# Two expert layers: every token through all eight experts, or each batch sorted by expert and only the chosen two computed

## The reference, cut to what matters

```python
logits = jnp.einsum('btd,ed->bte', x, router_w)          # 8 experts
top_vals, top_idx = jax.lax.top_k(logits, 2)
top_w = jax.nn.softmax(top_vals, axis=-1)
h = jnp.square(jax.nn.relu(jnp.einsum('nd,edh->enh', xf, w1)))   # 128 -> 256
y = jnp.einsum('enh,ehd->end', h, w2)                            # 256 -> 128
y_sel = y[idx_f, jnp.arange(N)[:, None]]
out = jnp.einsum('nk,nkd->nd', w_f, y_sel)                       # the two chosen
```

## Time and profile before

| | us |
|---|---|
| median of 3 runs | 1289.06 (1288.54 to 1292.21) |
| the profiled execution | 1291.25 |
| its span, first to last instruction | 1289.5 |
| granted TensorE clock, mean share of full | 0.96 |

### The profile page before, as it was taken

The page is one execution under the profiler, slowest core; times in us unless marked ns, Lnnn a source line. Parts: engine busy times, 40 slices in busy tenths (PEclk is TensorE's granted clock), DMA queues, the critical chain, the costliest instruction groups (busy, mean ns, idle before and its releaser), DMA issues.

```text
span 1289.5 us, 25719 instructions
## 1 busy us (share of the span) xinstructions
PE 1197.6 (93%) x10019; PEld 742.1 (58%) x10019; DVE 976.4 (76%) x2357; ACT 960.9 (75%) x1826; POOL 285.5 (22%) x326
## 2 busy tenths in 40 slices
PE   1779999998899999999999999999999999999998
PEld 1369999987434434444444444444444348999998
DVE  7575677766888898989898888988889814565654
ACT  1037777765158998888898888988888996777775
POOL 2032000003423333332332333332322100000000
PEclk9679999999569999999999999999999999999999
DMA  5100000000000000000000000000000000000000
GB/s 193 36 1 1 1 1 1 2 1 1 1 1 1 2 1 2 2 1 2 2 2 1 2 2 1 2 1 2 1 2 1 1 2 1 9 17 9 10 9 17
DMA packets 6134, 11.08 MB, mean 9 GB/s; under 512 B 1907, under 2 KB 3574, under 8 KB 5878
## 3 DMA queue, kind: packets, MB, share of 16 engines
q1 hardware_dynamic: 6014, 9.45, 2.1%
HBM read 7.28 MB, written 2.10 MB: 7 GB/s over the span
## 4 chain that ended last, share of the span: by engine, by line
PE 78%; DVE 13%; ACT 6%; issue 3%; DMA 0%; SPq 0%; ACTq 0%; DVEq 0%
PE acc L1280 17%; PE six L1115 17%; PE six L1251 10%; DVE mxp L947 8%; PE six L1103 6%; PE six L1105 5%; PE six L1104 5%; PE misc L1251 5%; ACT PB L645 3%; PE six L1264 2%; PE six L1217 1%; ACT SC L634 1%; PE six L1127 1%; PE six L1212 1%; PE misc L1103 1%
## 5 line engine op out<-in xcount | busy, mean ns | idle before, releaser
L947 DVE TENSOR_REDUCE mxp<-six 128x2 f32<-128x1024 f32 x512 | 598.8, 1219 | 75.4 <-PE six L1264 73.4
L645 ACT ACTIVATE PB<-six 128x512 f32<-128x512 f32 x681 | 384.9, 599 | 60.7 <-PE six L1251 36.9
L1280 PE MATMUL acc<-PB,Vg 128*32 128x256 f32 x4096 | 328.0, 392 | 16.3 <-ACT SC L634 16.3
L1264 PE MATMUL six<-K,Q 32*128 32x512 f32 x1024 | 264.1, 519 | 14.4 <-DVE mxp L947 9.7
L1251 PE MATMUL six<-Q,K 32*128 32x512 f32 x681 | 272.5, 498 | 0.1
L1115 PEld LDWEIGHTS six<-w2s,PB 128*128 128x128 f32 x2048 | 248.2, 192 | 11.3 <-ACT PB L547 0.7
L1115 PE MATMUL six<-w2s,PB 128*128 128x128 f32 x2048 | 249.3, 275 | 0.1
L850 DVE SCALAR_TENSOR_TENSOR x<-six,wexp,x 128x128 f32<-128x128 f32 x512 | 144.2, 345 | 134.9 <-PE six L1115 134.2
L541 ACT ACTIVATE PB<-six 128x512 f32<-128x512 f32 x256 | 151.2, 599 | 114.8 <-PE six L1105 104.4
L645 ACT ACTIVATE PB<-misc 128x512 f32<-128x512 f32 x343 | 205.4, 599 | 23.2 <-PE six L1251 17.1
L1251 PEld LDWEIGHTS six<-Q,K 32*128 32x128 f32 x681 | 107.9, 183 | 142.7 <-ACT PB L645 73.4
(11 more groups left out here) (225 smaller groups left out, 1094.7 us busy)
## 6 DMA issues: line engine op xcount, KB each, us to landing
x<-in_x SPq DMA_DIRECT2D x4, 512.0 KB, 5.1
SC<-in_w_om SPq DMA_DIRECT2D x1, 2048.0 KB, 14.6
out<-x SPq DMA_DIRECT2D x8, 256.0 KB, 2.0
VH<-in_w SPq DMA_DIRECT2D x1, 1024.0 KB, 9.2
Vg<-in_wqs SPq DMA_DIRECT2D x1, 256.0 KB, 8.0
Vg<-in_wks SPq DMA_DIRECT2D x1, 256.0 KB, 7.4
cst<-in_cst SPq DMA_DIRECT2D x1, 81.5 KB, 3.4
nwb<-in_nw SPq DMA_DIRECT2D x1, 64.0 KB
```

Of the source, the lines that this page charges most:

```text
L645: act.activation(PB[:, s % 3, j, :], scores, ACT.Exp).then_inc(G_("act_taken"), 1)
L947: dve.reduce_max(dst, taken_slot("max", s, i).rearrange("p (a n) -> p a n", a=2), AX.X).then_inc(G_("max_taken"), 1)
L1264: ins = pe.matmul(slot[:, c * BLK:(c + 1) * BLK], Q[rows, G % NG, t * P:(t + 1) * P], K[rows, G % NG, th * BLK:(th + 1) * BLK], start=True ...
L1280: ins = pe.matmul(acc[RB * j:RB * (j + 1), n], Vg[:, G % 2, t, j, :], PB[:, s % 3, j, n], start=(t == 0 and half == 0), stop=(t == TPB - 1 ...
```

## The change

Each expert layer now takes a whole batch (1024 tokens) at a time and computes only the two chosen experts.

**Routing a batch** (`rows`, `batch_top_two`, `batch_rank`, `batch_places`, `batch_weights`). VectorE normalises the 8 x 128 rows into `hbs`, TensorE turns them and multiplies with the router, VectorE takes the best two. TensorE counts with nine products (a triangle of ones, `tri`, and `ones`) how many (token, expert) pairs stand ahead of each pair, and VectorE computes from that a place in a list that is sorted by expert and in which each expert starts at a multiple of 128. The list has RT = 23 tiles of 128 lines, which is enough for 2 x 1024 pairs with any choice. POOL then sends the rows with 16 indirect DMAs of 128 rows (64 KB) each to `xs` in device memory (`send`), whose lines were set to zero before.

**The tiles.** SyncE loads the 23 tiles back in 6 groups (`load_lines`). TensorE turns each tile, multiplies it with the `w1` of the tile's expert (one fp32 product of 256 columns), turns the result (two transposes) and multiplies with `w2` (two fp32 products of 128 columns). Which expert that is, TensorE reads from memory into registers (`find_experts`, a TENSOR_LOAD for 4 tiles), and these address the weights. The tiles go in 12 pairs a batch, 48 steps a layer, with relu on VectorE (`relu_pair`) and the square and copies on ScalarE. SyncE stores the results to `yd` (`keep_lines`).

**Results.** POOL fetches them with 16 indirect DMAs a batch (`fetch_batch`), and VectorE adds them with their weights (`add_results`, 16 instructions of 128 columns a batch).

**Where it stands.** In the first layer batches 0, 1 and 2 are routed before the first tile (`experts_begin`), batch 3 beside the tiles of batch 0. The results of batches 0 and 1, attention's statistics for them and its first two norms and four projections lie beside the tiles of batches 2 and 3; the results of batches 2 and 3 are added within attention (`late_results`). In the second layer batches 0 and 1 are routed beside the last group of attention (`routed_late`), 2 and 3 beside the first tiles. `attention_end` now stands ahead of the second layer, with nothing beside it. Results of batches 1 to 3 are added after the last tile.

`w1` is no longer split and is loaded later, and the three-product form is gone from the experts (attention keeps it).

```diff
+RT = (2 * L + E * (P - 1)) // P
+TG = 4
+RGROUPS = -(-RT // TG)
+PAIRS = -(-RT // 2)
...
+            def send(f, b):
+                n = sparse_index(f, b)
+                pl.wait_ge(G_("dest_ready"), n + 1)
...
+                for i in range(TPB):
+                    for k in range(2):
+                        pl.indirect_dma_start(xs[b], bass.IndirectOffsetOnAxis(ap=dest[:, b, k, i:i + 1], axis=0),
+                                              hbs[:, b, i, :], None).then_inc(G_(f"sent{b}"), 16)
...
             low_part(2, 0)
-            split_out(0, 0)
             low_part(2, 1)
-            for t in range(1, 4):
+            fetch_start(0, 2)
+            for i in range(4):
+                fetch(0, 2, i)
+            for t in range(4):
                 split_out(0, t)
+            for i in range(4, TPB):
+                fetch(0, 2, i)
+            fetch_batch(0, 3)
             pl.wait_ge(*act_taken("v", 1))
...
-            low_part(3, 0)
-            for n in range(1, NBLK):
-                low_part(3, n)
+            for b in range(B):
+                send(1, b)
+            for b in range(B):
+                fetch_batch(1, b)
...
+            def experts_begin():
+                rms_norm(*RMS_GROUPS[0])
+                rms_norm(*RMS_GROUPS[1])
+                rows(0, 0)
+                rms_norm(*RMS_GROUPS[2])
+                batch_top_two(0, 0)
+                batch_weights(0, 0)
+                batch_places(0, 0)
+                rows(0, 1)
+                rms_norm(*RMS_GROUPS[3])
+                batch_top_two(0, 1)
+                rows(0, 2)
+                batch_places(0, 1)
+                batch_weights(0, 1)
+                batch_top_two(0, 2)
+                batch_places(0, 2)
+                batch_weights(0, 2)
...
+            def lines_hidden(f, b, q):
...
+                for r in range(2 * q, min(RT, 2 * q + 2)):
+                    ins = pe.matmul(big[:, n % 2, r % 2 * HID:(r % 2 + 1) * HID],
+                                    hTs[:, group % 2, r % TG * P:(r % TG + 1) * P], w1s[:, ds(expert_at[b, r], HID)],
+                                    start=True, stop=True)
...
+                for s in range(PAIRS * B):
+                    b, q = divmod(s, PAIRS)
+                    if q % 2 == 0 and s + 2 < PAIRS * B:
+                        turn_lines(f, *divmod(s // 2 + 1, RGROUPS))
+                    elif q % 2 and s + 3 < PAIRS * B:
+                        find_experts(f, *divmod((s + 3) // 2, RGROUPS))
+                    lines_hidden(f, b, q)
+                    if s:
+                        units_turned(f, *divmod(s - 1, PAIRS))
+                    if s >= 2:
+                        lines_result(f, *divmod(s - 2, PAIRS))
...
             pe.wait_ge(G_("max_taken"), len(DR))
+            for e in range(6):
+                attention_end(e)
             experts(1)
```

796 lines of the change are left out of this document (537 added, 259 removed).

## The result

The changed kernel takes **1270.77 us** (median of 3 runs, 1270.16 to 1273.85) against 1289.06: the ratio is 0.9858, with a 95% interval of 0.9823 to 0.9892. It is faster, by 18 us (1.4%) where 47 were forecast. A second measurement of the same kernel gave 1272.63, ratio 0.9865 (0.9845 to 0.9884). The profiled execution spans 1272.0 us. On other chips variants of this kernel are much slower than the kernel before; the last experiments are about that.

What follows compares the result with a forecast made beforehand. TensorE was taken to bound the expert layers and attention. Front +42, first layer -78, lead-in +9, attention +12 and second layer -32 sum to -47 us on a 1289.5 span: 1242 us, range 1190 to 1310.

Steps and rivals of the forecast that it cites:

- Attention, the step that failed: Attention's last group: two routings add 9.2 us to a nearly full TensorE, ScalarE's copies fall away, so 4 us.
- Attention, the lumps: Attention: VectorE's additions and statistics come in lumps longer than two PSUM slots cover (2.4 us), 1 us each, 8 us.
- (a): Expert layers: 24 register loads a layer at 0.7 us each cost 17 us, with 0 to 48 possible.
- (b): Expert layers: register instructions beside each pair's products cost 0.2 us a pair, 9 us a layer, with 0 to 47 possible.
- register work is hidden: Rival, expert layers: register loads and instructions fall to a third or nothing, -35 to -52 us, 1190 to 1207; chance 0.15.
- register work stalls TensorE: Rival, expert layers: loads at 2.0 us and 0.57 us a pair more, 96 us, giving 1338 us; chance 0.09.
- The layers: Expert layers: 106 us of tile products instead of 205; with additions, first layer 149 us (was 227), second 153.
- The front: Before the first tile: VectorE's norms start at 67.6, 5.5 us of waits for TensorE; 136 us (was 94, +42).
- the rule that spoke against it: POOL's row DMAs: VectorE's fast-mode copies block their descriptors, so sends beside applies and statistics become dearer.
- POOL as the bound: Rival, second layer: 112 row DMAs at c us each bound it; break-even about c = 1.75, 1334 us at 2.0; chance 0.13.
- Lead-in: Before attention: TensorE waits 6.5 us for POOL's fetches and maxima, plus 2.2 for adding half a batch on VectorE; +9 us.
- The rival on the other side: Slower side: POOL becomes the bound in the second layer if row DMAs cost 2.0 us each, 1334 us; chance 0.13.

Runs made afterwards that it cites:

- the last experiments: Variants of the changed kernel timed on other chips: 1412 to 1446 us on three of five, 1231 to 1282 on two; the kernel before 1289 to 1290.
- wide2: Changed kernel with the routing's narrow products widened to 128 columns (192 for the first rank product), same number and order: 1250.03 us, ratio 0.9689.
- static2: Changed kernel with a fixed expert for every tile, so no register loads or register instructions between products: 1440.21 us, on a chip with stalls.
- early2b: Changed kernel with the second layer's batches 2 and 3 routed four steps earlier, batch 2's rows normalised in attention's last group: 1257.31 us, ratio 0.9746.

## Why the prediction was wrong where it was wrong

The sign and the range held (1190 to 1310); the size did not. By its steps:

- **Attention, the step that failed.** "In the last group TensorE gets two routings (9.2 us) and is already busy 33.9 of 35 (the last of the earlier trace rows); ScalarE's copies fall away there, so 4 us." The 9.2 us were right (10 in wide2), the 4 should have been 10, since nothing gave way on a full TensorE. The other 17 us are the clock, which the sum didn't have there at all: I had looked at it after pauses and in the tiles, and took a busy TensorE for a safe one. The third row shows 1.00 in that group, and the earlier trace rows narrow products at the same clock, half as many instructions; but behind them, from 1067.65 on, the trace of before has products of 512 columns, not more narrow work and transposes. Of the 40 us missed, this is 23.
- **Attention, the lumps.** "The lumps are longer than two PSUM slots cover (2.4 us): 1 us each, 8 us." The waits were of that size (7.4 us); the stretches at 0.50 behind them made 16.5 of 8 (half-groups 1 to 12). The term was mis-sized by the same omission. Together 31 of the 40 us. The other 9 are attention's first half-group, 36.5 us from the first score product for 27 before: the second of the four additions stands in it, and the clock was 0.63 there, for 0.80; no run took that half-group apart.
- **Register work.** (a) 17 and (b) 9 us a layer were under 1 us where static2 took them out. My rival "register work is hidden" was right (0.15), and its own condition, a queue that runs ahead, is what the trace shows. The Trainium skill, page Runtime: NRT & Kernel Launch, section Instruction fetch mechanics, gives about 200 ns a register, by estimate 0.8 us for four; the trace has 0.33. The price of the rival "register work stalls TensorE" has a slip: 0.57 us more a pair would be 26 us a layer; its 17 belong to 0.57 us in all, 0.2 of them already counted.
- **The layers.** 106 us of products were 111: a steady pair is 2.20 us and half of a set of line transposes 0.22, times 46. With that and without (a) and (b) the first would be 128 and took 144: waits and a clock of 0.94, not 0.99, are 16 us. The second took 131, near 132 by the same sum.
- **The front.** +42 was +48. VectorE's norms started at 69.1 (forecast 67.6), and its waits were 12.8 us in all, 10.9 for TensorE and 1.8 for ScalarE, not 5.5, TensorE's mean clock being 0.61 from 66 to 142 us.
- **Row DMAs.** 1.2 us each; the trace has 1.25 to 1.26 from start to start (0.95 busy, 0.30 between). They kept that pitch beside VectorE's applies and additions too, at most 1.48 us in a run, so the rule that spoke against it cost nothing visible. POOL as the bound: not at c = 1.75, but 8 us of it at the tail were there, because batch 2's places came late. I had added 112 DMAs from the end of attention and overlooked that POOL stands idle for 33.5 us until 1142.3. Tail 29, measured 40; with early2b 33.4.
- **Lead-in.** TensorE's wait for POOL's maxima was 4.5 us (6.2 in the second profile), forecast 6.5; the stage grew by 4.4 us, not 9, since the addition on VectorE was covered.
- **The rival on the other side** had POOL's DMAs too dear. On three of five chips the sign did turn for the variants, by a mechanism that no term or rival had: not what a row DMA costs POOL, but what long runs of them do to the other engines, TensorE's late raises first. No row of before could show it, since that kernel has no row DMAs.

## What to carry to other kernels

A full engine is not a fast one: with every piece of TensorE work that is moved between others, ask for the granted clock behind it, not only for its length. Widening a narrow product costs next to nothing where both take nearly the same time (16 instructions of 8 columns took 1.85 us in the tiles, of 128 columns 1.95) and was worth 23 us by the medians here. Small-step work of VectorE belongs beside a bound engine in pieces that its buffers cover, each waiting for the last one rather than for itself. And a kernel that issues row DMAs from POOL in long runs should be timed on more than one chip.

## What the runs showed of the hardware that was not expected

- In attention's last group TensorE went from 1.00 to 0.50 behind eight products of 8 columns, fully busy, and stayed there for over 40 us on work that had held 1.00 before; with the same products at 128 columns it stayed at 1.00. Beside the tiles the same narrow products left it at 1.00.
- The same kernel takes 1250 us on one chip and 1437 on another, with the kernel before at 1290 on both; 2 us of pause after every fourth row DMA gave back 107 us on the slow kind. The Trainium skill, page DMA: Bandwidth & Descriptors, section Queues, rings and completion order, says that a DMA engine goes round the queues it has work for, a packet each. By that rule a page of instructions would not wait for a run of 40 us to end. On the slow kind none came for 50 to 56 us around such runs, but the engines stood still for much of that time, so this doesn't contradict the rule. What is recorded late are TensorE's raises of semaphores, by up to 36 us.
- A register load of four values takes 0.33 us on the weight-loading queue and costs nothing in a steady state of 2.20 us a pair (2.42 with the line transposes).
